# Spreading softmax reciprocals over the rows by DMA instead of by 0/1 products

## The reference

```
q = rms_norm(x @ q_w)                      # the the x rows are layer-normed first
img = context[:, :257]; txt = context[:, 257:]        # 1601 context rows per batch
k, v, k_img, v_img = projections of txt and img, k's rms-normed
out = (softmax(q k^T) v + softmax(q k_img^T) v_img) @ o_w    # 16 heads of 32
x1 = x + out;  h = layer_norm(x1)
FFN(h): router picks 4 of 32 experts per token (capacity 80 rows per expert),
        silu(h Wg) * (h Wu) @ Wd for each expert, plus the same with shared weights
```

## Time and profile before

| | |
|---|---|
| time, median of 3 runs | 1213.53 us (1213.5 to 1214.07) |
| span of the profiled execution | 1212.8 us |
| TensorE busy | 1150.7 us (95%) |
| VectorE busy | 824.9 us (68%) |
| ScalarE busy | 649.5 us (54%) |
| GpSimd busy | 190.7 us (16%) |
| granted TensorE clock, mean | 0.994 |
| bytes moved by DMA | 143.02 MB |

### The profile page before, as it was taken

One profiled execution on the slowest core, in us unless ns is written; L12 is line 12 of the kernel. 1 busy time (PEld: TensorE's weight loads), 2 busy tenths in 40 slices (PEclk: granted clock), 3 DMA queues, 4 the chain that ended last, 5 costly groups with the idle time before them and its releaser, 6 DMA issues. The chain is left out here.

```text
span 1212.8 us, 20795 instructions
## 1 busy us (share of the span) xinstructions
PE 1150.7 (95%) x8484; PEld 415.6 (34%) x8484; DVE 824.9 (68%) x1042; ACT 649.5 (54%) x916; POOL 190.7 (16%) x299
## 2 busy tenths in 40 slices
PE   6899999999999999999999999998999998999996
PEld 2342222444222244422224442222454433333332
DVE  6776878877677887768788777997778852222221
ACT  5558997444899744499864459885121121222221
POOL 1220000143000014300001430001110012333342
PEclk9999999999999999999999999999899999999998
DMA  9851000559200045910004693013823317999742
GB/s 312 178 113 36 2 2 10 131 119 211 36 2 2 11 129 135 205 26 2 2 26 114 147 195 111 2 36 106 329 75 121 115 59 289 357 317 317 243 62 33
DMA packets 140056, 143.02 MB, mean 118 GB/s; under 512 B 107952, under 2 KB 108208, under 8 KB 134960
## 3 DMA queue, kind: packets, MB, share of 16 engines
q1 hardware_dynamic: 134832, 130.78, 36.9%
q0 software_dynamic: 5120, 10.82, 4.7%
HBM read 95.67 MB, written 20.73 MB: 96 GB/s over the span
## 5 line engine op out<-in xcount | busy, mean ns | idle before, releaser
L665 ACT ACTIVATE work<-ps 128x1024 f32<-128x1024 f32 (+1 forms) x416 | 403.0, 1021 | 42.5 <-PE ps L1152 38.8
L1158 PE MATMUL ps<-work,vals 128*32 128x512 f32 (+2 forms) x1664 | 221.0, 603 | 1.2 <-ACT work L665 0.6
L994 PE MATMUL ps<-wts,work 128*128 128x512 f16 x864 | 193.1, 379 | 2.7 <-DVE work L721 2.4
L1152 PE MATMUL ps<-quer,keys 32*128 32x512 f16 x2496 | 171.9, 378 | 16.0 <-ACT work L665 2.8
L900 DVE TENSOR_TENSOR work<-work 128x2048 f32<-128x2048 f32 x64 | 146.6, 2291 | 6.3 <-DVE work L897 0.5
L900 DVE TENSOR_TENSOR attn<-attn,work 128x2048 f32<-128x2048 f32 x62 | 142.0, 2290 | 5.2
L994 PEld LDWEIGHTS ps<-wts,work 128*128 128x128 f16 x864 | 83.8, 98 | 109.7 <-issue 8.3
L1961 PE MATMUL ps<-wring,xgt 128*80 128x512 f32 x256 | 114.9, 592 | 0.0
L586 ACT CAST work<-work 128x512 f16<-128x512 f32 x68 | 42.0, 618 | 130.8 <-DVE work L753 130.8
L994 PE MATMUL ps<-wts,hl 128*128 128x512 f16 x432 | 100.2, 383 | 11.6 <-DVE wts L703 7.5
L1152 PEld LDWEIGHTS ps<-quer,keys 32*128 32x128 f16 x2496 | 46.2, 92 | 185.1 <-ACT work L665 159.9
(11 more groups left out here) (216 smaller groups left out, 1364.7 us busy)
## 6 DMA issues: line engine op xcount, KB each, us to landing
wring<-in_wx SPq DMA_DIRECT2D x32, 1536.0 KB, 8.9
raw<-in_ctx SPq DMA_DIRECT2D x52, 256.0 KB, 3.1
work<-in_x SPq DMA_DIRECT2D x4, 1024.0 KB, 5.3
table<-nums SPq DMA_DIRECT2D x16, 256.0 KB, 2.5
work<-in_x SPq DMA_DIRECT2D x12, 256.0 KB, 5.1
x<-work SPq DMA_DIRECT2D x12, 256.0 KB, 2.6
x2t_rows<-nums SPq DMA_DIRECT2D x12, 256.0 KB, 2.5
x2t<-x2t_rows SPq DMA_DIRECT2D x3, 1024.0 KB, 9.2
```

The source lines that it names most:

```text
L665: act.activation(prob[0:rows, s % PROBS, 2 * half:2 * half + 2, :], ps[0:rows, 2 * pair:2 * pair + 2, :], ACT.Exp, scale=SCALE).then_inc(a ...
L994: mm = pe.matmul(out, lhs(a, c)[:, cols], wts[:, w, z, c * D:(c + 1) * D], start=(k == 0), stop=(k == len(steps) - 1))
L1152: mm = pe.matmul(ps[:, 2 * pair + h % 2, :], k[h * HD:(h + 1) * HD, :], q[h * HD:(h + 1) * HD, :], start=(e == 0), stop=(e == len(terms) - 1))
L1158: return pe.matmul(ps[h * HD:(h + 1) * HD, NUM, :], vals[a:z, ORDER[n], g * P + h * HD:g * P + (h + 1) * HD], prob[a:z, s % PROBS, h, :], ...
```

## The change

1. The 0/1 matrices `sel` and the products with them are gone. SyncE stores `rcp` to DRAM (`store_sums`) and reads it back into SBUF with each row repeated over 32 partitions (`spread`), two groups of heads per transfer of 1 MB. At a change of batch both transfers use one buffer, `rb`; the second waits until the first two groups are weighed. After the last batch they use a buffer of their own, `rbl`, with no such wait.
2. `weigh` reads the reciprocals from SBUF. It begins in slot 2 instead of slot 1 (`WEIGH`), and the output products, residual, normalisation and stores move one slot on.
3. TensorE makes three shared gate products (gate 0, up 0, gate 1) ahead of the branch, and no 0/1 product. In the FFN program the gates come ahead of, or between, the weighing and the normalisation on ScalarE and VectorE, and expert loads 2 and 3 wait for the last weighing (`t_at`).
4. ScalarE's waits at the start of the exponentials for two kinds of stores move to VectorE, to the start of groups 0 and 1. A few semaphores are merged.

```diff
-O_SLOT = [6, 7, 10, 11]
+O_SLOT = [7, 8, 11, 12]
-NORM_SLOT = [8, 9, 12, 13]
-LOW_SLOT = [9, 10, 13, 14]
+NORM_SLOT = [9, 10, 13, 14]
+LOW_SLOT = [10, 11, 14, 15]
+WEIGH = 2
...
-        self.sel = at("sel", 172 * KB_, [P, NG, 2, P], F32)
+        self.rb = at("rb", 172 * KB_, [P, 2, 2, L], F32)
+        self.rbl = at("rbl", 164 * KB_, [P, NG, 2, L], F32)
...
+            def store_sums(bb):
+                sp.wait_ge(a_rcp, bb + 1)
+                sp.dma_start(r_dram[bb], rcp[:, :]).then_inc(s_rd, 16)
+
+            def spread(dst, bb, pair):
+                rows = r_dram[bb].rearrange("(h r) q -> h r q", h=4)[:, 4 * pair:4 * pair + 4, :]
+                return sp.dma_start(dst.rearrange("p g t q -> p (g t) q"), rows.unsqueeze(1).to_broadcast([4, HD, 4, L]))
+
+            def spread_pair(bb, q, pair):
+                if pair == 0:
+                    sp.wait_ge(s_zero, 32)
+                    sp.wait_ge(s_rd, 16 * bb)
+                    upto(sp, a_at, q * NG)
+                else:
+                    sp.wait_ge(a_at, gn(q, 1))
+                spread(rb[:, :, :, :], bb - 1, pair).then_inc(s_rb, 16)
+
+            def last_spreads(bb):
+                store_sums(bb)
+                sp.wait_ge(s_rd, 16 * (bb + 1))
+                for pair in range(2):
+                    spread(rbl[:, 2 * pair:2 * pair + 2, :, :], bb, pair).then_inc(s_rl[pair], 16)
...
+                        if i == 1 and b > 0:
+                            store_sums(bb - 1)
                         if i >= 1:
                             turn_key(bb, i - 1)
+                        if i in (1, 4) and b > 0:
+                            spread_pair(bb, q, i // 4)
...
             def weigh(q, g):
 
-                dve.wait_ge(a_sel, gn(q, g))
-                image = own(dve.tensor_tensor(nums[:, g, 1, :], nums[:, g, 1, :], ps[:, NUM, :], ALU.mult))
-                dve.tensor_tensor(nums[:, g, 0, :], nums[:, g, 0, :], ps[:, DEN, :], ALU.mult).then_inc(a_mt, 1)
+                dve.wait_ge(s_rb, 16 * (2 * q + g // 2 + 1))
+                image = own(dve.tensor_tensor(nums[:, g, 1, :], nums[:, g, 1, :], rb[:, g % 2, 1, :], ALU.mult))
+                dve.tensor_tensor(nums[:, g, 0, :], nums[:, g, 0, :], rb[:, g % 2, 0, :], ALU.mult).then_inc(a_mt, 1)
...
-                    if b > 0 and 1 <= i < 1 + NG:
-                        weigh(q, i - 1)
-                    if b > 0 and 2 <= i < 2 + NG:
-                        out_low(q, i - 2)
+                    if b > 0 and WEIGH <= i < WEIGH + NG:
+                        weigh(q, i - WEIGH)
+                    if b > 0 and WEIGH + 1 <= i < WEIGH + 1 + NG:
+                        out_low(q, i - WEIGH - 1)
...
-                    for k, (c, a, z) in enumerate(steps):
-                        pe.matmul(ps[:, GATE_BANK, :], swt[SG][:, a, c * D:c * D + P], m.x2t[0][:, :, z, c, :],
-                                  start=(k == 0), stop=(k == len(steps) - 1))
-                    pe.wait_ge(a_rcp, bb + 1)
-                    for t, bank in ((1, SEL_BANK[0][0]), (0, SEL_BANK[0][1])):
-                        pe.matmul(ps[:, bank, :], sel[:, 0, t, :], rcp[:, :], start=True, stop=True)
+                    gate(SG, 0, 0)
+                    pe.wait_ge(f_wlo, 3 * p + 2)
+                    gate(SU, 0, 2).then_inc(s_gate, 1)
+                    gate(SG, 1, 1)
...
             dve.memset(ia[:, :], 0.0).then_inc(s_const, 1)
+            gate(0)
             weigh(0)
+            gate_low(0)
             weigh(1)
+            gate(1)
             out_low(0)
             weigh(2)
             out_low(1)
+            gate_low(1)
             weigh(3)
...
-            for g in range(1, NG):
-                spread(g)
-            gate_up(0)
-            pe.wait_ge(t_mt, 2)
             gate_up(1)
+            gate_up(2)
+            gate_up(3)
             for j in range(QT):
                 output(j)
```

More of the change, by code:

```diff
@@ L479, in _ @@
                 sp.wait_ge(s_turned[1], 64)
+                for pair in range(2):
+                    sp.wait_ge(s_rl[pair], 32)
             sp.end_ifs()
@@ L879, in sums_and_results @@
                         ffn_weight(p, g - 1)
+                    if b > 0 and g < 2:
+                        for j in range(2):
+                            dve.wait_ge((s_tab, s_x2)[g][j], 16 * ((out_batch(bb - 1) + 1) * QT // 2))
                     dve.wait_ge(a_img, gn(bb, g))
@@ L982, in _ @@
                 one_pass(1)
+                for pair in range(2):
+                    dve.wait_ge(s_rl[pair], 32)
             dve.end_ifs()
@@ L1063, in value @@
                             parts={6: weights(bb // B, 2)} if bb % B == 0 and k == 0 else None).then_inc(v_mm, 1)
-            def spread(bb, q, g):
-                if g == 0:
-                    pe.wait_ge(a_nt, gn(bb, NG - 1))
-                    pe.wait_ge(a_rcp, bb + 1)
-                else:
-                    pe.wait_ge(a_mt, gn(q, g - 1))
-                for t, bank in ((1, NUM), (0, DEN)):
-                    mm = pe.matmul(ps[:, bank, :], sel[:, g, t, :], rcp[:, :], start=True, stop=True)
-                mm.then_inc(a_sel, 1)
             def output(q, j):
@@ L1095, in project @@
                         value(bb, KV_AT[i - 1])
-                    if b > 0 and 1 <= i < 1 + NG:
-                        spread(bb - 1, q, i - 1)
                     if b > 0 and i in O_SLOT:
@@ L1473, in gate_tanh @@
             def gate_tanh(n):
-                act.wait_ge(f_gu, n + 1)
+                if n == 0:
+                    act.wait_ge(s_gate, 1)
+                else:
+                    act.wait_ge(f_gu, n)
                 upto(act, f_t, n)
@@ L1491, in norm_store @@
                          ps[:, TURN_BANK[j], :].bitcast(F16)).then_inc(n_out, 1)
-            for g in range(NG):
-                out_high(g)
             gate_tanh(0)
             gate_high(0)
+            out_high(0)
             gate_tanh(1)
+            out_high(1)
             gate_high(1)
+            out_high(2)
+            out_high(3)
+            gate_tanh(2)
+            gate_high(2)
+            norm_high(0)
+            norm_high(1)
+            gate_tanh(3)
+            norm_high(2)
+            norm_high(3)
+            gate_high(3)
             for j in range(QT):
-                norm_high(j)
-            for j in range(QT - 1):
                 norm_store(j)
-            gate_tanh(2)
-            norm_store(QT - 1)
-            gate_high(2)
             act.wait_ge(e_r, 1)
@@ L1508, in _ @@
                            scale=-1.0 / WS).then_inc(e_ez, 1)
-            for n in range(3, 13):
+            for n in range(4, 13):
                 gate_tanh(n)
@@ L1669, in _ @@
             out_norm(1)
+            gate(3)
             out_rows(2)
@@ L1675, in _ @@
             out_norm(3)
+            gate_low(3)
             norm_low(3)
-            gate(2)
             dve.wait_ge(s_const, N_CONST)
@@ L1815, in product @@
                 return mm
-            def spread(g):
-                image, text = SEL_BANK[g]
-                if g == 3:
-                    pe.wait_ge(t_mt, 1)
-                pe.matmul(ps[:, image, :], sel[:, g, 1, :], rcp[:, :], start=True, stop=True)
-                pe.matmul(ps[:, text, :], sel[:, g, 0, :], rcp[:, :], start=True, stop=True).then_inc(t_sel, 1)
             def output(j):
@@ L2016, in build @@
         s_xr = ctx.enter_context(nc.semaphore("s_xr"))
-        attention_program(nc, m, d, x1_dram, x2_dram, table, out, s_turned, s_xr)
-        ffn_program(nc, m, d, x1_dram, table, out, s_turned)
+        s_rl = [ctx.enter_context(nc.semaphore(f"s_rl{g}")) for g in range(2)]
+        s_gate = ctx.enter_context(nc.semaphore("s_gate"))
+        attention_program(nc, m, d, x1_dram, x2_dram, r_dram, table, out, s_turned, s_xr, s_rl, s_gate)
+        ffn_program(nc, m, d, x1_dram, table, out, s_turned, s_rl, s_gate)
 def kernel(**inputs):
```

116 lines of the change are left out of this document (55 added, 61 removed).

## The result

The changed kernel takes 1339.88 us (median of four runs, 1334.85 to 1346.91) where the kernel before takes 1213.8 beside it: a ratio of 1.104, 95% interval 1.099 to 1.109. That is slower, as forecast, but outside the range of 1222 to 1292: 126 us were lost where 58.6 were foretold. The profiled execution, the shortest of the four (1334.85 us), has a span of 1333.0 us against 1212.8, 120.2 more.

The account below looks back on a forecast made before the run. TensorE was 95% busy, but VectorE's order decides at changes of batch: three losses of 18.5 us (55.5) plus FFN 3.1 make 58.6 over 1212.8, with 0.7 for the median 1272 us; own range 1255 to 1292, whole 1222 to 1292.

Parts of the forecast that it names:

- W1: Change of batch, slot 2: VectorE stands 8.3 us before weigh(0) until the first spread lands.
- W2: Change of batch, slot 4: VectorE stands 13.7 us before weigh(2), 1.3 us of transpose issue plus the second spread's landing.
- FFN part: From the branch on: later branch, removed products and waits of 2.0 and 2.8 us for spreads, net +3.1 us.
- start-up: Kernel start: eight small copies for the 0/1 matrices go, but VectorE waited for the first weights after them, so nothing.
- The landing time L: A 1 MB spread, cut along its outermost count of 4, keeps to four engines and lands in 12.4 us.
- 26.8 GB/s per engine: Spreads: each of four engines moves its 256 KB at the rate seen with all engines full, 9.8 us.
- The bound of 22.4: Spread's landing, upper bound: four times a 256 KB repeated-row load's 5.6 us; rival of slow repeated reads, about 1340 us, chance 0.04.
- The store of rcp: Change of batch: SyncE's 256 KB store of the reciprocals lands in 2.6 us, before the first spread is issued.
- The two places of waiting: Change of batch: VectorE waits before weigh(0) in slot 2 and weigh(2) in slot 4, 8.3 and 13.7 us.
- VectorE's slots bind without waits: Change of batch: without either wait VectorE's 7 us slots bind, so the gain is 3.5 us, not 8.6.
- Weigh from SBUF costs the same: Weighing on VectorE: reading reciprocals from SBUF instead of PSUM still takes 0.69 us.
- the hidden rival: Spreads land before the weighs want them, L below 2.2 us: gains 3 x 3.5 and 1.7, 1201 us, chance 0.11.

Follow-up runs that it names:

- e4: Changed kernel without the spreads or any wait for them, weighing with bias rows already there (normalisation left out): 1209.6 us.
- e3: Changed kernel with spreads reading 128 different rows in a row, outermost count 128, instead of repeated rows (normalisation left out): 1243.4 us.
- e6: Changed kernel with each spread as four transfers, one per 32 partitions, each in four blocks of 8, so four engines write partitions 8 apart: 1305.6 us.
- b1: Changed kernel with 16-block spreads of 512 KB per group into alternating buffers, issued early, the reciprocals' store ahead of the x loads: 1230.7 us.
- e7: Changed kernel with the second spread issued one slot earlier, ahead of key 3's transpose: 1320.2 us.
- e13: Changed kernel with the six spreads of the changes of batch issued by GpSimd in its own queue, still awaited, everything computed: 1343.0 us.
- e5: Changed kernel with the six spreads of the changes of batch issued but not awaited, normalisation of three batches left out: 1315.5 us.
- e9: Changed kernel with each spread as one transfer whose source is cut in 8 blocks of 16 repeats instead of 4 of 32: 1286.4 us.
- e8: Changed kernel with each spread as one transfer whose source is cut in 16 blocks of 8 repeats instead of 4 of 32: 1257.9 us.
- e12: As e5, unawaited, but the six spreads of the changes of batch are issued by GpSimd into its own DMA queue: 1272.6 us.
- b2: As b1, with the second spread of the FFN part issued behind the branch instead of ahead of it: 1227.2 us.
- e1: Changed kernel with each spread cut into four 256 KB transfers, one per head group, whose source starts with the 32 repeats: 1256.7 us.
- e10: As e8, 16 blocks, but reading different rows instead of repeated ones (normalisation left out): 1257.7 us.
- e2: Changed kernel with spreads reading four blocks of 32 different rows instead of repeated rows (normalisation left out): 1337.8 us.

## Why the prediction was wrong in size

| term of the sum, us | predicted | measured |
|---|---|---|
| wait in slot 2, W1 | 8.3 | 14.6 (17.17, 12.60, 14.05) |
| wait in slot 4, W2 | 13.7 | 18.7 (19.08, 18.30, 18.76) |
| what is gained without them | -3.5 | -1.9 (e4) |
| clock and the rest | 0 | +1.0 (difference) |
| per change | 18.5 | 32.4 |
| three changes | 55.5 | 97.2 |
| FFN part | 3.1 | 24.2 |
| start-up | 0 | -1.2 |
| sum | 58.6 | 120.2 |

*The landing time L* is the step that failed. "Four engines carry 256 KB each" held (share 0.23 to 0.28), "26.8 GB/s per engine" did not: it was read from a stretch in which all engines run plain 128-partition loads, and e3, a plain transfer to 128 partitions, has that rate too (24.9). With the destinations 8 apart e6 lands in 13.2 us, near my 12.4, and takes 1305.6. So 4.2 of the 5.0 us that L was too small, in both waits of each change, go with partitions 32 apart being written together. Of the 61.6 us between the two sums, L makes about 46: 10 in each change and 15.6 in the FFN part. Even the upper end of my own range (L = 15.1) lay below 17.4; the bound of 22.4 was given too small a weight.

*The store of rcp* was to land in 2.6 us, as x stores do; it took 5.2 (median of four), because it stands behind 1.5 MB of x and residual loads just issued. Ahead of them it takes 2.2 (b1). So the first spread was issued 9.0 us after the start of the reciprocal, not 7.2. With the 5 us of L, and VectorE coming 0.6 us later, W1 is 6.3 us too small.

*The two places of waiting* were right, and so was the reason for the second (e7). *VectorE's slots bind without waits* was right in kind (e4: 1.9 of 7.7 us come back). *Weigh from SBUF costs the same* was right (688 ns).

*What queues behind the spread* was missing. I listed what stands behind the waiting instruction on VectorE, not what stands behind the transfer on its DMA engines. It cost little here, as it lies beside the wait (e13), but it makes the hidden rival wrong: I had it decided by L and the order, and e5 with no wait at all is still 25.4 us per change. Its 1201 us was out of reach besides; the floor is 1209.6.

*The FFN part* was 21 us too small. The flag product came 8.2 us after the reciprocal (8.1 predicted, 5.3 before). The branch took VectorE 8.4 us, not 5.9, but the wait for the first spread covers that. The waits are 6.3 and 12.1, not 2.0 and 2.8: the first spread landed in 19.0 us (12.4 predicted), the second 18.8 behind it (9.8). So the output products start 51.3 us after the last reciprocal (987.08), not 35.7: 15.6 of the 21 us. Most of the rest lies between them and the router's exponential (25.7 us, 21.2 predicted). Without spreads the tail is +0.2 (e4), so the gates ahead of the branch cost nothing in sum.

*The slow clock* after each standstill was not in the sum: 12 matmuls take 1.5 us more, twice per change. What is left of that in the total isn't measured; all that the other terms don't explain is 1.0 us per change. *Start-up* gained 1.2 us where I had nothing.

Left open: why the packets of the changed kernel are slow for part of the time only (17 GB/s per engine, 14 in e9 and e8), and why the start is 1.2 us shorter.

## What to carry to other kernels

Before a row is repeated over partitions by DMA, look at the outermost count of the source and at which partitions the engines then write in step: the same 1 MB landed in 17.4, 13.2, 7.3 or 5.4 us. Then list what is issued behind that transfer in the same queue: loads there landed about when the transfer did. And ask what the removed work was worth where it stood: 23 us of TensorE products were worth 6 us here, at the floor.

## What the hardware showed that I had not expected

- A load issued 0.6 us behind a four-engine transfer took 18 us instead of 3.2, and a transpose held its issuer for 9.1 to 11.4 us instead of 1.24 (e5). With the transfer in GpSimd's own queue the load's 18 became 9.5 to 10.4 us (e12).
- Packets of 8 KB took 309 ns, or about 600 where the cut makes two engines write 32 partitions apart.
- The gap of the branch on VectorE was 5.3 us without spreads, 5.9 before, 7.5 with one spread of sixteen blocks ahead of it and 10.8 with two (b2, b1; 10.7 to 11.2 in e1, e8 and e10). With two plain ones it was 8.0 (e3), with two on four engines 7.6 to 9.4. The page lists two queues of kind "instruction" (68 and 35 packets), so the FFN program's instructions may come through the same DMA engines; b1 against b2 shows the dependence, not the mechanism.
- Reading the same DRAM rows 8 or 32 times cost nothing (e10 against e8, e2 against the changed kernel).
